# A delta-rule chain whose first product is split into two column tiles, with V's scaling and the seed product moved

## The reference, cut to what matters

```python
q, k, v = (silu(conv4(x @ W)) for W in (Wq, Wk, Wv))     # 16 heads of 16
q, k = l2norm(q) / 4, l2norm(k);  beta = sigmoid(x @ Wb)
def step(S, inp):                                         # 512 steps, S: [2, 16, 16, 16]
    u = vt - einsum('bhk,bhkv->bhv', kt, S)
    S = S + bt * kt[..., :, None] * u[..., None, :]
    o = einsum('bhk,bhkv->bhv', qt, S)
o = rmsnorm(o) * sigmoid(x @ Wg) @ Wo
```

## Time and profile before

| | us |
|---|---|
| median of 3 runs | 879.14 |
| lowest and highest | 877.88, 885.92 |
| the profiled execution, device time | 881.38 |
| its span in the trace | 879.6 |
| elimination to the last copy into `ftc` | 71.0 to 109.1 |
| units 0 to 3 and seed | 109.1 to 118.4 |
| chain, first load of chunk 0 to that of chunk 31 | 118.4 to 215.1 |
| rows to the experts on POOL | 235.0 to 254.3 |

### The profile page before, as it was taken

The page is one execution under the profiler, slowest core; times in us unless marked ns, Lnnn a source line. Parts: engine busy times, 40 slices in busy tenths (PEclk is TensorE's granted clock), DMA queues, the critical chain, the costliest instruction groups (busy, mean ns, idle before and its releaser), DMA issues.

```text
span 879.6 us, 12287 instructions
## 1 busy us (share of the span) xinstructions
PE 830.1 (94%) x4287; PEld 586.5 (67%) x4287; DVE 469.0 (53%) x1062; ACT 317.8 (36%) x655; POOL 177.8 (20%) x263
## 2 busy tenths in 40 slices
PE   5897798999998999899999999998999999999998
PEld 3375666777656778577777776776766655565557
DVE  5969966675742224775564566557534252232223
ACT  3768566655513334343324234323222211111111
POOL 3668253411340007011111111111100000000000
PEclk9979989999999999999999999999999999999999
DMA  4002094027134323012110101010123334444431
GB/s 137 1 2 40 10 344 135 2 60 211 60 116 148 108 67 97 13 49 84 43 36 25 36 25 37 25 37 25 37 80 126 113 126 125 139 143 125 128 112 48
DMA packets 63956, 72.05 MB, mean 82 GB/s; under 512 B 14200, under 2 KB 48504, under 8 KB 63768
## 3 DMA queue, kind: packets, MB, share of 16 engines
q1 hardware_dynamic: 59048, 64.06, 24.1%
q0 software_dynamic: 1536, 4.20, 1.5%
q10 hardware_dynamic: 3312, 3.02, 1.0%
HBM read 55.45 MB, written 14.75 MB: 80 GB/s over the span
## 4 chain that ended last, share of the span: by engine, by line
PE 77%; DVE 11%; issue 5%; ACT 3%; POOL 2%; DMA 1%; SPq 0%; DVEq 0%; ACTq 0%; POOLq 0%
PE bank L920 9%; PE bank L878 9%; PE bank L896 9%; PE bank L1094 8%; PE bank L1061 7%; PE bank L959 6%; PE bank L945 6%; PE bank L627 3%; PE bank L1796 3%; PE bank L649 2%; PE bank L1758 2%; PE bank L1782 2%; PE bank L1654 2%; POOL rows_in L830 2%; DVE arena L2144 1%
## 5 line engine op out<-in xcount | busy, mean ns | idle before, releaser
L1123 ACT ACTIVATE arena<-bank 128x512 f32<-128x512 f32 (+1 forms) x64 | 34.7, 544 | 217.6 <-PE bank L878 217.5
L1231 DVE TENSOR_TENSOR arena<-arena,bank 128x512 f32<-128x512 f32 (+1 forms) x47 | 30.7, 653 | 151.8 <-PE bank L896 151.8
L920 PE MATMUL bank<-arena 128*128 128x256 f32 x448 | 107.4, 380 | 1.0 <-DVE arena L1229 0.9
L878 PE MATMUL bank<-xnT,arena 128*128 128x512 f32 (+1 forms) x256 | 107.0, 540 | 0.0
L896 PE MATMUL bank<-xnT,arena 128*128 128x512 f32 (+1 forms) x256 | 106.7, 539 | 0.0
L920 PEld LDWEIGHTS bank<-arena 128*128 128x128 f32 x448 | 84.9, 191 | 31.0 <-issue 20.0
L1192 ACT ACTIVATE arena<-bank 128x512 f32<-128x512 f32 (+1 forms) x96 | 46.8, 524 | 135.5 <-PE bank L1061 135.5
L846 POOL TENSOR_TENSOR arena<-arena,causal_t 128x256 f32<-128x256 f32 x64 | 45.0, 725 | 247.3 <-ACT arena L1197 247.3
L896 PEld LDWEIGHTS bank<-xnT,arena 128*128 128x128 f32 x256 | 48.8, 190 | 47.5 <-issue 45.8
L1094 PEld LDWEIGHTS bank<-arena 128*128 128x128 f32 x640 | 76.3, 192 | 4.3 <-POOL arena L846 2.9
L1094 PE MATMUL bank<-arena 128*128 128x129 f32 x640 | 77.0, 275 | 1.9 <-POOL arena L846 1.9
(11 more groups left out here) (237 smaller groups left out, 1243.7 us busy)
## 6 DMA issues: line engine op xcount, KB each, us to landing
arena<-in_w_gu SPq DMA_DIRECT2D x60, 256.0 KB, 3.6
rows_in<-place SPq DMA_DIRECT2D x5, 1664.0 KB, 14.5
arena<-in_w_dn SPq DMA_DIRECT2D x56, 128.0 KB, 3.5
arena<-in_wq SPq DMA_DIRECT2D x32, 128.0 KB, 2.2
arena<-in_wo SPq DMA_DIRECT2D x32, 128.0 KB, 2.0
arena<-cw_rows SPq DMA_DIRECT2D x15, 256.0 KB, 3.7
arena<-rows_in SPq DMA_DIRECT2D x23, 128.0 KB, 2.0
rows_out<-arena ACTq DMA_DIRECT2D x23, 128.0 KB, 1.7
```

What stands on the lines that cost most here:

```text
L878: mm = nc.tensor.matmul(ring(M)[0][:, 0:n], w_gu[:, slot_of(M), k * P:(k + 1) * P], xnT[:, k, cols], start=(k == 0), stop=(k == KD - 1))
L920: mm = nc.tensor.matmul(Y[s][half][l // 2][:, (l % 2) * DIM:(l % 2 + 1) * DIM], hh[:, M % 3, j * P:(j + 1) * P], w_dn[:, slot_of(M), :], s ...
L1123: nc.scalar.activation(sg[:, M % 2, 0:n], ring(M)[0][:, 0:n], ACT.Silu).then_inc(s_silu, 1)
```

## The change

It has three parts.

1. L1782's product is written as two for each q, one for each batch: a 128x64 stationary operand by 64 moving columns, output to partitions 0 to 63 for batch 0 and 64 to 127 for batch 1. The blocks where the batches differ aren't computed any more. So a chunk has 16 matmul records of 64 columns in place of 8 of 128. L1796 stays as it is.
2. V's scaling leaves POOL's place ahead of the units. Tile 0 is scaled by DVE (two operations of 128x256) between the elimination and L2244; tiles 1 to 3 by POOL behind its spreads 3, 5 and 7 (two operations of 128x256 each). All engines' waits on DVE's count go up by 2, and PE's units 4, 8 and 12 wait for the tile's scaling.
3. The seed product goes ahead of units 0 to 3 on PE, behind a wait for all of `ftc`.

```diff
             def units(i): ...
-                        pe.wait_ge(s_rv, 4)
+                        pe.wait_ge(s_el, el_n + 2)
                         pe.wait_ge(s_fta, 8)
+                    if i >= 4 and i % 4 == 0:
+                        pe.wait_ge(s_rv, t)
...
-            for i in range(4):
-                units(i)
+            pe.wait_ge(s_fta, 8)
             pe.wait_ge(s_seed, 1)
             for h in range(2):
                 nc.tensor.matmul(sacc[h][:, 0:256], ident[:], seed, start=True, stop=False, skip_group_check=True)
+            for i in range(4):
+                units(i)
...
-                        mm = nc.tensor.matmul(uo[h][s][:, j * P:(j + 1) * P],
-                                              xy_at(c, hq), sh[:, hq, :],
-                                              start=(par == 0 and j == 0), stop=(par == 1), skip_group_check=True)
+                        for b in range(BATCH):
+                            o = slice(b * 64, b * 64 + 64)
+                            mm = nc.tensor.matmul(uo[h][s][o, j * P + b * 64:j * P + b * 64 + 64],
+                                                  xy_at(c, hq)[:, o], sh[:, hq, o],
+                                                  start=(par == 0 and j == 0), stop=(par == 1), skip_group_check=True)
...
         # pool
-            for i in range(4):
-                pool.wait_ge(s_siv, KD + i + 1)
-                v = rt[:, 2 * i:2 * i + 2, :, D0:32].rearrange("p n h d -> p (n h) d")
-                nc.gpsimd.tensor_tensor(v, v, wz[:, 2 * i * H0:(2 * i + 2) * H0].unsqueeze(2).to_broadcast([P, 32, D0]),
-                                        ALU.mult).then_inc(s_rv, 1)
...
+            def scale_v(t):
+                pool.wait_ge(s_siv, KD + 4)
+                for b in range(BATCH):
+                    n = b * 4 + t
+                    ins = nc.gpsimd.tensor_tensor(rt[:, n, :, D0:32], rt[:, n, :, D0:32],
+                                                  wz[:, n * H0:(n + 1) * H0].unsqueeze(2).to_broadcast([P, H0, D0]), ALU.mult)
+                ins.then_inc(s_rv, 1)
+
             for i in range(NFI):
                 spread(i)
+                if i in (3, 5, 7):
+                    scale_v((i - 1) // 2)
...
         # vector
+            dve.wait_ge(s_siv, KD + 4)
+            dve.wait_ge(s_srk, 2)
+            for n in (0, 4):
+                nc.vector.tensor_tensor(rt[:, n, :, D0:32], rt[:, n, :, D0:32],
+                                        wz[:, n * H0:(n + 1) * H0].unsqueeze(2).to_broadcast([P, H0, D0]), ALU.mult).then_inc(s_el, 1)
             dve.wait_ge(s_ft, 8)
```

## The result

| | before | after |
|---|---|---|
| median of 20 runs, us | 882.04 | 877.63 |
| lowest and highest, us | 877.70, 886.16 | 870.53, 882.75 |
| profiled execution, device time / span, us | 881.38 / 879.6 | 872.18 / 870.2 |
| mean granted clock of the profiled execution | 0.984 | 0.990 |
| first load of chunk 0, of chunk 31, us | 118.4, 215.1 | 112.65, 207.71 |

After to before is 0.9944 (95% interval 0.9919 to 0.9968). That is 4.4 us less in the medians: less than the bound of 1% that the prediction set for a difference, though the interval excludes 1.

The account below looks back on a forecast made before the run. Bound: a chain of waits, by PE in even chunks below 24, as closely by DVE in odd ones, by ACT's copies ahead. 3.6 + 0.38 - 0.1 = 3.9 us off 879.14 gives 875.3; range 873.5 to 877.5, wide 870.5 to 881.0.

Parts of the forecast that it names:

- rival A: Units ahead of the chain: the moved seed makes the clock rise sooner, giving 874.1 or 873.5 us; chance 0.20.
- Rival C: Chain: less busy PE lets the clock fall, up to 3.2 us each; one fall 878.5, two 881.7; chance 0.10.
- Part 1, even chunks: Even chunks with a unit: column tiles end each half 0.27 us earlier, none in chunk 20; 2.97 us won.
- Rival B: L1782's product: the tiles don't overlap at 64 columns, so they win nothing and drains cost; 880.6 us; chance 0.09.
- Part 1, odd chunks: Odd chunks below 24: DVE's copy can't start before L2271 is done, so PE's saving becomes slack; gain 0.
- Rival D: Odd chunks gain too, 3.2 us, if DVE's copy can go ahead of L2271; 872.1 us; chance 0.06.
- Part 1, the other chunks: Late chunks and those following full-width work: 0.4 us won in 28 to 30, 0.2 in 15, 23 and 31.
- Part 2: Ahead of the chain: elimination ends 3.3 us earlier, but ACT's copies hold the stage; only the 0.38 us gap is won.
- The contention with the scaling: A DVE spread beside POOL's moved scaling, perhaps in chunk 1, is held: 0.1 us lost, bounds 0 and 0.85.
- Part 3: Seed ahead of unit 0 fills PE's wait of 2.39 us: gain 0, bounds 0 and 0.5 lost.

Follow-up runs that it names:

- e3: After, with DVE's `xye` additions moved from behind the even chunk's masking to behind the odd chunk's copies: 876.06 us, ratio 0.9927 to before.
- e1: The kernel before with the column tiles of L1782's product and nothing else: 881.51 us, ratio 0.9981 to before.
- e6: The kernel before with the column tiles alone, plus unread products in PE's waits of six chunks: 887.75 us, ratio 0.9963 to before.
- e7: The kernel before with the column tiles alone, run a second time, on another chip: 893.33 us, ratio 1.0019 to before.
- e8: After unchanged, run again on a third chip: 889.19 us, ratio 0.9957 to before.
- e2: After with the first product whole again, so the kernel before with V's scaling and the seed moved: 880.61 us, ratio 0.9973 to before.
- e10: After with `xye` behind the odd chunk's copies and unread products in PE's waits, both in the chain and ahead of it: 886.12 us, ratio 0.9906 to before.
- e4: After with the seed product back behind units 0 to 3: 878.12 us, ratio 0.9943 to before.
- e5: e3 with POOL's scaling of tile 1 behind its spread 4 in place of 3: 885.53 us, ratio 0.9943 to before.

## Why the prediction was right, and where it was not

**The total.** Forecast: 3.9 us less, measured 4.4 less (0.9919 to 0.9968 of 882.04: 2.8 to 7.1). The time of 877.63 is 2.3 over the 875.3 of the forecast, 0.1 over its narrow range and inside the wide one of 870.5 to 881.0. The 2.3 come from the median of three from which 3.9 was subtracted: 879.14 was itself 2.9 under the median of twenty. The size is right in part by luck: the profile shows two effects that stood as rivals, A and C, with opposite signs, and the terms of the sum were off in both directions. The prediction also said that a granted clock of 0.50 inside the chain would make it wrong. There was one, and the total held all the same, as one stretch cost only 1.25 us.

**Part 1, even chunks: right in sum.** By 16 loads in 0.76, chunks 2, 4 and 6 gained the forecast 0.26 to 0.27 each. The others differ: 0.34 in chunk 0, 0.43 in 8, 0.58 in 16 (which follows full-width work), and only 0.17 or 0.18 in 10, 14, 18 and 22. The ten even chunks below 24 other than 12 and 20 gained 2.83, chunk 12 another 0.26 where no fall came, chunk 20 nothing: 3.09 where 2.97 was booked. That the sum fits so well is partly luck, as more and less than 0.27 cancel. Rival B is out.

**Part 1, odd chunks: right.** 2.51 before and after in chunk 5, and DVE's copy still 0.82 behind the load. e3 shows the reason that was given: taking L2286 out of the way gives 0.30 for each. Rival D is false for the change, and describes e3.

**Part 1, the other chunks: the wrong term.** Booked were 0.4 won in 28 to 30, 0 in 24 to 27, 0.2 in 15, 23 and 31, and 0 in 13 and 21. Measured, periods in us:

```
chunk    13    15    21    23    24    25    26    27    28    29    30
before  2.61  2.99  2.61  2.74  2.58  2.96  2.89  3.07  3.83  2.55  3.74
after   2.81  2.93  2.81  2.38  2.78  2.76  3.09  3.27  3.68  2.49  3.84
```

24 to 30 lost 0.3 together, and 28 to 30 alone won 0.1. Chunk 15's gain of 0.06 is the forecast 0.07; chunk 23 won 0.36. What was missed: the price of a change between full width and tiles was applied to the chunks where PE is late, and not to those where the full-width product had been hidden under DVE's masking. Timeline of after at the end of chunk 13:

```profile
153.82 0.87 DVE L2322 TENSOR_TENSOR sh<-bank,hdiag 128x256 f32<-128x256 f32 x2 [0.60 <-PE bank L1801]
153.95 0.47 PEld L1828 LDWEIGHTS bank<-ident,arena 128*128 128x128 f32 x4
154.06 0.60 PE L1828 MATMUL bank<-ident,arena 128*128 128x128 f32 x4
154.59 0.55 PEld L1787 LDWEIGHTS bank<-sh,arena 128*64 128x64 f32 x16 [0.17 <-issue]
```

The load comes 0.07 before the end of L1828 (154.66), 0.77 behind the start of L2322. In the kernel before it came at 160.95, 0.58 behind the same start (160.37), while the full-width product ran until 161.22. That is 0.19 lost, and the periods of chunks 13, 21, 24 and 27 show 0.20 each. The same rule gave the right price; the list of the places was too short. Chunk 26 lost 0.20 too, in the kernels that have the moves, and not with the tiles alone (2.89 in e1, e6 and e7). What does that stays open.

The chain in sum: 96.69 before, 95.06 after. The fall cost 1.25 (chunk 11 with 4.24 and chunk 12 with 3.67, against 3.60 and 3.06 in profiles without it), so 93.8 without it: 2.9 won, where 3.3 to 3.6 were forecast. e8, whose chain had no fall, took 93.81. The tiles alone come to 3.1 when their falls are taken out (93.6). Their full-clock time, 4.0 and 4.6 less, is somewhat more than that; where the rest lies, I can't say.

**Part 2: the stage right, its size too small.** ACT did hold the stage: DVE's elimination got 2.64 us earlier against the end of the copies (4.06 for 1.42), and only the gap was won. The rows had shown 0.38 of gap; the copies' stage, from the first L1738 to the end of the last copy, went from 8.16 to 7.48, which is 0.68. But the tiles alone had 7.48 too in both their profiles (e1, e7), with V's scaling still on POOL, and 8.14 in e6. In e1 and e7 stretches at 0.50 had put PE's work back, L1738 started at 103.11 and 106.17 (100.88 before, 97.54 in e6), and the elimination was done in time. So this gain is there only in executions in which PE comes early. DVE's two new operations took 0.76 (forecast 0.88), POOL's 1.2 for a pair (forecast 1.5). The contention with the scaling, priced at 0.1, cost DVE 0.28 in e2, within its bound of 0.85, though ahead of the chain and not in chunk 1. The prediction didn't look at POOL's own spreads: when the units run at full clock, these hold DVE's without a pause, and the twelve take 5.96 and 5.99 us (e2, e10). From the last copy to chunk 0 are then 8.4 and 8.5 us, and 7.7 to 7.9 in the profiles with a short stretch at 0.50, so the faster units gained nothing there.

**Part 3: "0" was wrong in the profile.** The seed gives nothing by itself, and its work does fill a wait. But the clock rose sooner with it, and the units took 4.75 us in place of 6.35, as e4 confirms (6.26 with the seed back behind them): rival A, which had 0.20. Its argument against it, that PE had been busy 2.08 of 3.40 us with no rise, counted the units alone. In after PE was busy for all 3.40 of the stretch from 105.50, seed and slowed units together.

**Rival C: it happened, and one stretch cost less than priced.** It had 0.10, and up to 3.2 us for a stretch, as it took the units' 6.35 us for the length. The stretches in the chain lasted 3.4 us and cost 1.2 to 1.5 each, 1.25 in the profile of after, so it decides nothing there. In the tiles alone the mean clock says 2.7 and 5.9 us, against 4.0 and 4.6 won; only the first is found in the chain. The prediction looked for the danger at 197.0 to 200.4, the chunk at which PE was less busy in a view of the late chain. All five chains with a fall have one in chunk 11 or 12, behind a wait of 1.5 us that the argument never looked at. A windows view over the whole chain would have shown 2.03 busy of 3.40 at 150.9 to 154.3, below the 2.50 that I took for the weakest point. But busy PE isn't the whole of it: the second falls of e1 and e5, late in the chain, came behind stretches with PE busy 3.09 of 3.40.

## What to carry to other kernels

Where a chain has waits on other engines, less work on TensorE can lower its clock. Look over all of the stage for PE's longest waits, and count a fall behind them as a risk with a price taken from the trace's own stretches at half the clock. A few unread products in such waits cost 1.6 us of full-clock time here, and with them the mean clock was back at that of the kernel before (0.9805 and 0.9799). Read span times mean clock beside the median, for kernels on one chip: it tells in a dozen runs whether the work shrank, even where the gate hides it. And when a product changes its tiling, list every full-width product that stands ahead of it in program order, hidden or not.

## What was not expected of the hardware

- Two kernels that differ in unread matmuls alone: the one with more of them was faster by 5.6 us (887.75 and 893.33), at a mean clock of 0.9805 and 0.9734. The traces account for 1.4 us of it in the chain.
- Nearly all of the spread between runs of a kernel is the clock: over after's 20 runs each us at 0.50 costs 0.48 us, and full-clock time scatters by 0.7.
- What POOL costs DVE depends on TensorE's clock: with faster units POOL doesn't pause, and DVE's twelve spreads take 5.96 us in place of 4.96 (0.34 us for one around a pause of POOL's, 0.56 beside its spreads, 0.70 beside its scaling).
